# One attention prologue, reordered: a second key stack made by a selector product, queries earlier, the second block's keys later

## The chip, the core and the metric

The program runs on one core of a Trainium2 chip. The metric is the device time of one execution in microseconds. Before the change three runs gave 613.34, 617.55 and 617.87 us, median 617.55 us. One more execution was profiled: it took 615.51 us, its span in the trace is 613.8 us.

The core has five engines with queues of their own: TensorE (PE; its weight loads are PEld), VectorE (DVE), ScalarE (ACT), GpSimd (POOL) and SyncE (SP), which here does nothing but issue DMAs. They meet only through semaphores.

## The reference

The input is 2048 tokens of 128 features. Two layers each add an attention-like branch and an FFN-like branch to the layer norm of the input. The change lies at the start of layer 0, in the branch with 16 query heads, 4 key/value heads and a head width of 8:

```
xn = layernorm(x)                      # (x - mean) / sqrt(var + eps)
h  = rmsnorm(xn) * ln1
q, k, v = h @ Wqkv + bqkv              # 16, 4 and 4 heads of 8
q, k = rmsnorm(rope(q)) * qn, rmsnorm(rope(k)) * kn
out  = softmax(causal(q k' / sqrt(8))) v   # all 2048 tokens
...                                    # gate, output product, mixture of 8 experts
```

The chunk-summary branch of layer 0 reads the same xn. Everything behind (experts, the state-space layer, the last FFN) is not touched.

## The kernel before, in words

**Blocks.** The 2048 tokens are 16 tiles of 128, and 4 blocks of 4 tiles. SP loads x block by block (line 676); the third block's load is issued behind eight smaller ones.

**Prologue on DVE.** For each block: `statistics` (lines 1745, 1748: four BatchNorm statistics, four aggregations), then ACT takes the root of the variance (line 896), DVE inverts it (1754), and `normed` computes the four tiles `xn = (x - mean) * rstd` with one tensor_scalar each (1756). Two small products (1758, 1759) lead to a second root on ACT (898) for the RMS scale. PE transposes the four tiles (1214), ACT copies the result to `xnT` (902), and PE multiplies it with the weights (1220) once DVE has scaled these by ln1 (1787). `bound_of_scores` (1767 to 1775) computes a few constants from the norm weights. `block_taken` (1794) reads the products out of PSUM, one tile per instruction. `rotated`, `keys_split` and `split` apply the rotary tables and the norms and write each number as a high and a low part. All this stands in one written order on DVE.

**Stacks.** A score product has 32 rows of contraction (8 numbers, split in four), and four of them run side by side in the array. So the queries of a group (4 heads that share one key head) and four copies of its keys lie stacked on 128 partitions, in `qst` and `kst`. The queries come stacked out of a transpose (1252). The keys come as four groups on 32 partitions each (`keysT`, transposed at 1245, copied by ACT at 923), and must be repeated four times. For group 0 of block 0 a product with a 32 by 128 selector does that (1309), and ACT copies its result (925). For all other groups and blocks SP does it by DMA, four DMAs per group (`spread_keys`, 714): 12 for block 0, 16 for each later block. `keysT` is one buffer: the next block's keys may be copied there once the last block's DMAs have landed.

**Steps.** The attention is a list of 136 steps `k`: (group, query block, key tiles). Query block 0 is steps 0 to 9: group 0 has steps 0 and 1, group 1 steps 2 to 4, group 2 steps 5 and 6, group 3 steps 7 to 9. Block 1 begins at step 10, and from step 14 on it uses its own keys. Each step is two score pieces on PE (1335), two exponentials on ACT of 1024 columns each (965), a causal mask on POOL where the tiles are diagonal (843; all of steps 0 to 9), and the value product on PE two steps later (1354). The score pieces go around three pairs of PSUM banks. The value products of two groups accumulate in bank 6; before the next pair may start there (step 5's product, issued in step 7), DVE must have copied the bank out (2070).

**Side tasks.** Beside the steps, PE works through one list of other products that share bank 7, at most one at a time, each at a step given by the `ASKED` table: the query stacks of the next groups (QUERIES), the transpose of the next block's keys (KEYS), the transposed sums (ATT, 1437), the projections of blocks 2 and 3 (QKV). PE starts one only when the one before has been read out of the bank, nearly always by DVE (2187 for QUERIES, 2182 for KEYS, 2210 and 2215 for ATT). DVE has a list of events sorted by a step number: reading the side tasks, and the block's own norm and rotation work (squares 2086, sums 1807, roots 1892 to 1897, rotation 1815 to 1818, `keys_split` 1826 to 1834, `split` 1840 to 1842, the chunk means 1880 and 1882). Both lists are fixed when the program is written: an engine that reaches an entry early waits.

In the kernel before, the side tasks of the first steps are QUERIES of group 1 at step 0, of group 2 at step 2, of group 3 at step 4, KEYS of block 1 at step 5, ATT at step 7, QUERIES of block 1, group 0 at step 8. Step 2 waits until the 12 DMAs have landed.

## Time and profile before

| | |
|---|---|
| runs | 613.34, 617.55, 617.87 us |
| profiled execution | 615.51 us, span 613.8 us |
| PE busy | 560.9 us (91%) |
| ACT busy | 460.6 us (75%) |
| DVE busy | 399.9 us (65%) |
| POOL busy | 123.0 us (20%) |
| mean granted TensorE clock | 0.986 |

How to read it: the shares are means over the whole program. The change touches roughly the first 55 us of it; what it is worth is decided by who waits for whom there, and by whether the stages behind simply begin earlier.

### The profile page before, as it was taken

Reading aid. Unit: us, or ns where it says so; the run is one execution under the profiler, and the core shown is the slowest. Engines: PE = TensorE matmul, PEld = TensorE weight load, DVE = VectorE, ACT = ScalarE, POOL = GpSimd, SP = SyncE. Lnnn points to the kernel's source line nnn. Section 1 sums busy time; section 2 is a strip of 40 time slices with the busy share of each in tenths; the row PEclk is TensorE's granted clock in tenths of the full one; section 3 lists DMA queues with packets and bytes.
Section 4 is the critical chain, followed back from the end, with each engine's and each line's share of the span. In section 5 each row is a group of like instructions: output and inputs, shape, how many; then the busy total and the mean of one; then the engine's idle time right before and its main releaser. Section 6 shows DMA issues by size and latency. Waiting matters only on the chain.

```text
span 613.8 us, 11144 instructions
## 1 busy us (share of the span) xinstructions
PE 560.9 (91%) x3912; PEld 330.6 (54%) x3917; DVE 399.9 (65%) x1060; ACT 460.6 (75%) x642; POOL 123.0 (20%) x160
## 2 busy tenths in 40 slices
PE   4578989999999999999997899799689999999998
PEld 3233335344344333433334568467468887887887
DVE  7986765737445242576534855789689788788673
ACT  2368988898989999998794456559777687686673
POOL 2044221011101012010630545303011001010010
PEclk9879999999999999999899899999999999999999
DMA  7112002013422220040135331300000000000000
GB/s 230 27 43 70 2 1 70 1 32 95 172 92 105 104 88 18 2 139 1 45 100 161 114 88 40 94 1 2 0 1 1 2 18 1 2 18 1 1 18 18
DMA packets 31174, 30.98 MB, mean 50 GB/s; under 512 B 6912, under 2 KB 21024, under 8 KB 31120
## 3 DMA queue, kind: packets, MB, share of 16 engines
q1 hardware_dynamic: 29872, 27.71, 14.4%
q0 software_dynamic: 1248, 2.57, 1.2%
q8 instruction: 32, 0.52, 0.4%
q14 instruction: 22, 0.18, 0.1%
HBM read 13.44 MB, written 12.89 MB: 43 GB/s over the span
## 4 chain that ended last, share of the span: by engine, by line
PE 68%; DVE 19%; issue 5%; ACT 4%; DMA 2%; SPq 1%; POOL 1%; DVEq 0%; ACTq 0%; POOLq 0%
PE ps L1354 18%; PE ps L1335 8%; PE ps L92 5%; PE ps L94 5%; PE ps L93 5%; PE ps L1654 2%; PE ps L1418 2%; PE ps L1431 2%; PE ps L1252 1%; PE ps L1529 1%; PE ps L1692 1%; PE ps L1695 1%; PE ps L1423 1%; SPq L714 1%; ACT r L965 1%
## 5 line engine op out<-in xcount | busy, mean ns | idle before, releaser
L965 ACT ACTIVATE r<-ps 128x1024 f32<-128x1024 f32 x272 | 258.0, 1036 | 29.4 <-PE ps L1335 27.3
L1354 PE MATMUL ps<-r 128*32 128x512 f32 (+3 forms) x1280 | 146.5, 544 | 2.2 <-DVE r L2070 0.9
L843 POOL TENSOR_SCALAR_AFFINE_SELECT r<-r 128x512 f32<-128x512 f32 (+1 forms) x80 | 47.3, 593 | 219.2 <-ACT r L965 218.9
L1335 PE MATMUL ps<-r2r 32*128 32x512 f32 (+3 forms) x640 | 78.1, 451 | 6.2 <-DMA r2r<-r2r 4.3
L1335 PEld LDWEIGHTS ps<-r2r 32*128 32x128 f32 x640 | 34.4, 184 | 47.7 <-ACT r L965 18.8
L886 POOL TENSOR_TENSOR r<-r 128x512 f32<-128x512 f32 x16 | 22.1, 1382 | 151.5 <-ACT r L1163 130.5
L1354 PEld LDWEIGHTS ps<-r 128*32 128x32 f32 x1280 | 27.8, 108 | 42.3 <-issue 29.8
L94 PE MATMUL ps<-r2r 128*128 128x512 f32 (+1 forms) x104 | 39.0, 375 | 0.0
L93 PE MATMUL ps<-r2r 128*128 128x512 f32 (+1 forms) x88 | 32.8, 372 | 0.0
L861 POOL DMA_INDIRECT rows_by_token<-r x23 | 26.3, 1145 | 18.9 <-ACT r L1018 10.3
L92 PE MATMUL ps<-r1r 128*128 128x512 f32 x64 | 26.3, 411 | 1.7 <-DVE r2r L2482 1.5
L821 POOL DMA_INDIRECT rows_by_expert<-r x16 | 15.7, 984 | 58.0 <-DVE r L1994 54.1
L94 PE MATMUL ps<-r1r,r2r 128*128 128x512 f32 x64 | 25.2, 394 | 0.0
L93 PE MATMUL ps<-r2r,r1r 128*128 128x512 f32 x64 | 25.2, 394 | 0.0
L1141 ACT ACTIVATE r1r<-r 128x512 fp32r<-128x512 f32 x16 | 10.1, 629 | 19.7 <-DVE r L2430 19.5
L1148 ACT ACTIVATE r<-ps,row 128x512 f32<-128x512 f32 x16 | 11.0, 687 | 16.6 <-PE ps L94 16.1
L92 PE MATMUL ps<-r2r 128*128 128x512 f32 (+1 forms) x56 | 20.9, 373 | 1.6 <-DVE r2r L2387 1.1
L94 PEld LDWEIGHTS ps<-r2r 128*128 128x128 f32 x104 | 19.6, 188 | 3.8
L1232 PE MATMUL ps<-consts 128*128 128x512 bf16 x69 | 18.0, 400 | 3.3 <-DMA r<-rows_by_token 1.4
L2495 DVE TENSOR_SCALAR r<-ps,r 128x128 f32<-128x128 f32 x64 | 17.9, 343 | 3.9 <-PE ps L1674 3.9
L2187 DVE CAST r2r<-ps 128x512 fp32r<-128x512 f32 x15 | 10.4, 691 | 14.7 <-PE ps L1252 14.5
L2013 DVE SCALAR_TENSOR_TENSOR r<-r,ps 128x256 f32<-128x256 f32 x23 | 9.7, 420 | 15.2 <-ACT r L943 15.0
(403 smaller groups left out, 1190.2 us busy)
## 6 DMA issues: line engine op xcount, KB each, us to landing
rows_by_expert<-r SPq DMA_DIRECT2D x34, 258.0 KB, 2.5
r2r<-r2r SPq DMA_DIRECT2D x60, 64.0 KB, 2.0
r<-in_f_W SPq DMA_DIRECT2D x1, 2048.0 KB, 9.3
r<-rows_by_expert SPq DMA_DIRECT2D x23, 64.5 KB, 1.8
res<-in_x SPq DMA_DIRECT2D x4, 256.0 KB, 4.5
r<-in_g_h1T SPq DMA_DIRECT2D x1, 1024.0 KB, 5.6
r<-in_g_h2T SPq DMA_DIRECT2D x1, 1024.0 KB, 7.8
r<-rows_by_token SPq DMA_DIRECT2D x4, 256.0 KB, 3.8
```

The costliest lines, as they stand in the source:

```text
L92: pe.matmul(dst, wh, xh, start=start, stop=False)
L93: pe.matmul(dst, wh, xl, start=False, stop=False)
L94: return pe.matmul(dst, wl, xh, start=False, stop=stop)
L821: pool.indirect_dma_start(hbuf, bass.IndirectOffsetOnAxis(ap=slot_u[:, i:i + 1], axis=0), h2_rows[i], None).then_inc(s_scat, 16)
L843: pool.affine_select(blk, blk, pattern, ALU.is_ge, nothing, base=0, channel_multiplier=-1).then_inc(s_msk, 1)
L861: pool.indirect_dma_start(tbuf, bass.IndirectOffsetOnAxis(ap=token_u[:, t:t + 1], axis=0), ysb[:, t, :], None).then_inc(s_ysc, 16)
L886: pool.tensor_tensor(mm[:, b], ed[:, b], along(gm[:, b, :], NH), ALU.mult).then_inc(s_cm, 1)
L965: act.activation(probs[:, n % PBUFS, :, :], ps[:, b:b + 2, :], ACT.Exp).then_inc(s_exp, 1)
L1232: pe.matmul(ps[:, bank, :], busy_w, busy_x, start=True, stop=True)
L1335: m = pe.matmul(ps[:, 2 * (n % SBUFS) + h, at:at + TB - query], kst[32 * j:32 * j + 32, group, P * kt:P * kt + P], qst[32 * j:32 * j + 32, ...
L1354: m = pe.matmul(ps[32 * j:32 * j + 32, 6, query:TB], vp[:, kt, group, :], probs[:, (2 * v + j // 2) % PBUFS, j % 2, at:at + TB - query], s ...
L2495: dve.tensor_scalar(ed[:, b, h, :], ps[:, 1, P * h:P * h + P], cums_f[:, NH * i + h:NH * i + h + 1], 0.0, ALU.subtract, ALU.min).then_inc( ...
```

## The change

- **Normalisation moves from DVE to ACT.** DVE computes `negmean = -mean * rstd` for the four tiles of a block with one small instruction; ACT computes `xn = Identity(rstd * x + negmean)` tile by tile, four activations with a scale and a bias column each.
- **The weights are scaled by ln1 on ACT**, behind the roots of block 1.
- **`bound_of_scores` is cut into three pieces** at three places of DVE's order.
- **Second key stack.** The selector is built for 64 rows, and a second selector product makes the stack of group 1 in bank 5; ACT copies it. The DMAs of block 0 are 8 instead of 12, and the wait for them moves from step 2 to step 5. On PE the first key stack now comes ahead of the first query stack.
- **Order in the tail of the prologue.** DVE reads two tiles of block 1, copies the first query stack, then reads the other two.
- **Side tasks.** QUERIES of groups 1, 2, 3 at steps 0, 1, 3 (were 0, 2, 4); KEYS of block 1 at step 8 (was 5, now behind ATT); QUERIES of block 1, group 0 at step 9 (was 8); DVE's `split` of block 1 at 8.2 (was 6.4), which puts the first chunk means (8.1) ahead of it. From step 10 on both lists are as before.
- **Filler products** (`kept_busy`) ahead of step 0: one instead of five.

```diff
-        key_rows = lambda b: 16 * (NQ - REP) + 16 * NQ * b
+        key_rows = lambda b: 16 * (NQ - 2 * REP) + 16 * NQ * b
...
-            + [(at, 1, "KEYS", b, None, 0) for b, at in ((1, 5), (2, 25.5), (3, 48))]
-            + [(2 * g - 2, 1, "QUERIES", (0, g), None, 0) for g in range(1, NKV)]
+            + [(at, 1, "KEYS", b, None, 0) for b, at in ((1, 8), (2, 25.5), (3, 48))]
+            + [(at, 1, "QUERIES", (0, g), None, 0) for g, at in ((1, 0), (2, 1), (3, 3))]
...
-               ((1, (8, 12, 16, 19)), ...
+               ((1, (9, 12, 16, 19)), ...
...
-            spread_keys(0, range(1, NKV))
+            spread_keys(0, range(2, NKV))
...
-            at = slice(0, 32)
-            step.alone(pool.tensor_copy(selk[at].rearrange("p (j y) -> p j y", j=REP), along(ident[at, at], REP)))
+            for at in (slice(0, 32), slice(32, 64)):
+                step.mark(pool.tensor_copy(selk[at].rearrange("p (j y) -> p j y", j=REP), along(ident[at, at], REP)))
+            step.settle()
...  ACT, block_roots(b)
+                act.wait_ge(s_nm, b + 1)
+                for i in range(TPB * b, TPB * b + TPB):
+                    act.activation(xn[:, i, :], res[:, i, :], ACT.Identity, bias=negmean[:, i:i + 1],
+                                   scale=rstd[:, i:i + 1]).then_inc(s_xn, 1)
...  ACT, behind block_roots(1)
+            act.wait_ge(s_wqkv, 16 * 5)
+            act.activation(wqkv, wqkv, ACT.Copy, scale=ln1).then_inc(s_wsc, 1)
...  ACT, behind the copy of the first key stack
+            act.wait_ge(s_skt, 2)
+            act.activation(kst[:, 1, 0:TB], ps[:, 5, :], ACT.Copy).then_inc(s_skc, 1)
...  PE
-            pe.wait_ge(s_xnTc, 1)
-            pe.wait_ge(s_split, 1)
-            queries_transposed(0, 0).then_inc(s_sqt, 1)
-            kept_busy(5, 2)
+            def keys_stacked(bank, g):
+                return pe.matmul(ps[:, bank, :], selk[32 * g:32 * g + 32, :], keysT[32 * g:32 * g + 32, :],
+                                 start=True, stop=True)
             pe.wait_ge(s_kc, 1)
             pe.wait_ge(s_sel, 1)
             pe.wait_ge(s_xnTc, 2)
-            pe.matmul(ps[:, 1, :], selk[0:32, :], keysT[0:32, :], start=True, stop=True).then_inc(s_skt, 1)
+            keys_stacked(1, 0).then_inc(s_skt, 1)
+            pe.wait_ge(s_split, 1)
+            queries_transposed(0, 0).then_inc(s_sqt, 1)
+            keys_stacked(5, 1).then_inc(s_skt, 1)
...  PE, k == 0
-                        kept_busy(5, 3)
+                        pe.wait_ge(s_xnTc, 3)
+                        kept_busy(2, 1)
...  PE, k == 1
+                        pe.wait_ge(s_skc, 2)
-                    elif k == of_round(1, 0)[0]:
+                    elif k == of_round(2, 0)[0]:
                         pe.wait_ge(s_krep, key_rows(0))
...  DVE, normed(b)
-                for i in range(TPB * b, TPB * b + TPB):
-                    dve.tensor_scalar(xn[:, i, :], res[:, i, :], mv[:, i, 0:1], rstd[:, i:i + 1],
-                                      ALU.subtract, ALU.mult).then_inc(s_xn, 1)
+                dve.scalar_tensor_tensor(negmean[:, at], mv[:, at, 0], -1.0, rstd[:, at], ALU.mult, ALU.mult
+                                         ).then_inc(s_nm, 1)
...  DVE
-            dve.wait_ge(s_wqkv, 16 * 5)
-            dve.tensor_scalar(wqkv, wqkv, ln1, None, ALU.mult).then_inc(s_wsc, 1)
             statistics(2)
             scales(0)
+            bound_of_scores(0)
             normed(2)
-            bound_of_scores()
...
             statistics(3)
+            bound_of_scores(1)
             normed(3)
             rotated(0, 1)
+            bound_of_scores(2)
...
-            block_taken(1)
+            block_taken(1, range(0, 2))
             dve.wait_ge(s_sqt, 1)
             dve.tensor_copy(qst[:, 0, 0:TB], ps[:, 0, :]).then_inc(s_sqc, 1)
+            block_taken(1, range(2, 4))
...
-            split_at.update({1: 6.4, 2: 24.6})
+            split_at.update({1: 8.2, 2: 24.6})
```

## Rows read from the trace of the kernel before

**Rows 1.** The page, chain of work that ended last, share of the span by engine.

```profile
PE 68%; DVE 19%; issue 5%; ACT 4%; DMA 2%; SPq 1%; POOL 1%; DVEq 0%; ACTq 0%; POOLq 0%
```

**Rows 2.** Timeline of ACT: start us, us, engine, line, operation, tiles, count, idle before.

```profile
31.23 3.77 ACT L965 ACTIVATE r<-ps 128x1024 f32<-128x1024 f32 x4 [0.64 <-PE ps L1335]
37.94 1.94 ACT L965 ACTIVATE r<-ps 128x1024 f32<-128x1024 f32 x2 [2.94 <-PE ps L1335]
...
54.92 22.79 ACT L965 ACTIVATE r<-ps 128x1024 f32<-128x1024 f32 x24 [0.15 <-PE ps L1335]
```

**Rows 3.** Third load of x: timeline of SP, then the DMA view (KB, us to landing).

```profile
4.78 0.99 SPq L676 DMA_DIRECT2D res<-in_x  x2
...
res<-in_x SPq DMA_DIRECT2D x1, 256.0 KB, 5.3
```

**Rows 4.** Timeline of the prologue, all engines.

```profile
10.31 0.87 DVE L1745 BATCH_NORM_STATS2 stats<-res 128x6 f32<-128x128 f32 x4
...
11.04 2.90 PE L1220 MATMUL ps<-r,xnT 128*128 128x192 f32 x8 [0.60 <-ACT xnT L902]
...
14.62 1.39 DVE L1794 SCALAR_TENSOR_TENSOR r<-ps,small,row 128x192 f32<-128x192 f32 x4
...
20.65 1.12 DVE L1756 TENSOR_SCALAR xn<-res,small 128x128 f32<-128x128 f32 x4
...
21.68 0.15 DVE L1758 TENSOR_TENSOR small<-small 128x4 f32<-128x4 f32 x1
```

**Rows 5.** ACT groups by form: count, busy us, mean ns, idle before us.

```profile
L1073 ACT ACTIVATE r<-r,row 128x512 f32<-128x512 f32 x5 | 3.9, 802 | 0.0
...
L955 ACT ACTIVATE r<-ps 128x128 f32<-128x128 f32 x5 | 1.4, 275 | 2.6 <-PE ps L1295 2.6
```

**Rows 6.** Timeline of the hand-over from prologue to steps.

```profile
27.85 0.42 DVE L1842 CAST r1r<-r1r 128x512 fp32r<-128x512 f32 x1
28.07 7.60 SPq L714 DMA_DIRECT2D r2r<-r2r  x12
...
31.13 0.66 PE L1252 MATMUL ps<-consts,r1r 128*128 128x128 f32 x4
...
31.89 0.69 DVE L2187 CAST r2r<-ps 128x512 fp32r<-128x512 f32 x1 [0.98 <-PE ps L1252]
```

**Rows 7.** Timeline of DVE in the first steps.

```profile
40.92 0.69 DVE L2187 CAST r2r<-ps 128x512 fp32r<-128x512 f32 x1 [1.17 <-PE ps L1252]
...
47.04 0.69 DVE L2187 CAST r2r<-ps 128x512 fp32r<-128x512 f32 x1
...
49.96 0.69 DVE L2070 COPY r<-ps 128x512 f32<-128x512 f32 x1 [0.79 <-PE ps L1354]
...
53.20 0.49 DVE L2215 TENSOR_TENSOR r<-ps,r 128x128 f32<-128x128 f32 x2
```

**Rows 8.** Timeline of PE and of SP: second spread, steps 10 and 14.

```profile
49.26 10.71 SPq L714 DMA_DIRECT2D r2r<-r2r  x16
...
50.70 1.06 PE L1354 MATMUL ps<-r 128*32 128x512 f32 x8 [0.21 <-DVE r L2070]
...
55.82 0.68 PE L1335 MATMUL ps<-r2r 32*128 32x512 f32 x4
...
63.83 0.51 PE L1335 MATMUL ps<-r2r 32*128 32x512 f32 x4
```

**Rows 9.** Windows: stretch, us, PE, PEld, DVE, ACT, POOL busy, PEclk, DMA.

```profile
34.50:35.00 0.50, 0.00 (x0) 0.00 (x0) 0.47 (x2) 0.50 (x1) 0.30 (x1) 0.68 0.39 98
...
41.00:41.50 0.50, 0.50 (x11) 0.28 (x12) 0.50 (x1) 0.00 (x0) 0.00 (x0) 0.50 0.00 0
```

**Rows 10.** Timeline of PE after the DMA wait.

```profile
37.10 0.80 PE L1335 MATMUL ps<-r2r 32*128 32x512 f32 x4 [4.29 <-DMA r2r<-r2r]
37.83 1.93 PE L1354 MATMUL ps<-r 128*32 128x512 f32 x8
```

**Rows 11.** Timeline of DVE: one operation of `keys_split`, block 0 and block 1.

```profile
25.63 0.29 DVE L1830 TENSOR_TENSOR r<-r,row 128x128 f32<-128x128 f32 x1
...
44.28 0.61 DVE L1830 TENSOR_TENSOR r<-r,row 128x128 f32<-128x128 f32 x1
```

More of the change, by code:

```diff
@@ L306, in build @@
         roots = small[:, 32:64].rearrange("p (q a i) -> p q a i", q=NB, a=2)
+        negmean = small[:, 112:128]
         inverse = small[:, 64:96].rearrange("p (q a i) -> p q a i", q=NB, a=2)
@@ L533, in build @@
             [(at + 2 * n, 2, "QKV", (b, n), None, 0) for b, at in ((2, 10), (3, 14)) for n in range(2)]
-            + [(at, 1, "KEYS", b, None, 0) for b, at in ((1, 5), (2, 25.5), (3, 48))]
-            + [(2 * g - 2, 1, "QUERIES", (0, g), None, 0) for g in range(1, NKV)]
+            + [(at, 1, "KEYS", b, None, 0) for b, at in ((1, 8), (2, 25.5), (3, 48))]
+            + [(at, 1, "QUERIES", (0, g), None, 0) for g, at in ((1, 0), (2, 1), (3, 3))]
             + [(at, 1 if b < 2 else 2, "QUERIES", (b, g), ("KEYS", b), 1) for b, steps in
-               ((1, (8, 12, 16, 19)), (2, (25.6, 33, 45, 52)), (3, (65, 74, 89, 102))) for g, at in enumerate(steps)]
+               ((1, (9, 12, 16, 19)), (2, (25.6, 33, 45, 52)), (3, (65, 74, 89, 102))) for g, at in enumerate(steps)]
             + [(27, 4, "KV", 0, ("KEYS", 2), 0), (26, 4, "GMAT", 0, ("KV", 0), 2), (31, 4, "G0", 0, ("KV", 0), 2),
@@ L1764, in scales, with bound_of_scores @@
                 step.alone(dve.reciprocal(hs[:, at], sd2[:, at]))
-            def bound_of_scores():
-                step.alone(dve.tensor_tensor(kw, qn_bc, kn_bc, ALU.mult))
-                step.mark(dve.tensor_scalar(kw, kw, QD ** -0.5, None, ALU.mult))
-                step.mark(dve.tensor_reduce(mx2[:, 0:1], qn_bc, X_AXIS, ALU.max, apply_absolute_value=True))
-                step.mark(dve.tensor_reduce(mx2[:, 1:2], kn_bc, X_AXIS, ALU.max, apply_absolute_value=True))
-                step.settle()
-                step.alone(dve.tensor_tensor(shift, mx2[:, 0:1], mx2[:, 1:2], ALU.mult))
-                step.alone(dve.tensor_scalar(shift, shift, -(QD ** 0.5), None, ALU.mult))
-                step.mark(dve.memset(qhl_f[:, :, :, 1, 1, 0], 1.0))
-                step.mark(dve.tensor_copy(khl[:, :, :, 1, 1, 0], shift.unsqueeze(2).broadcast_to([P, TPB, NKV])))
+            def bound_of_scores(piece):
+                if piece == 0:
+                    dve.wait_ge(s_wqkv, 16 * 5)
+                    step.mark(dve.tensor_tensor(kw, qn_bc, kn_bc, ALU.mult))
+                    step.mark(dve.tensor_reduce(mx2[:, 0:1], qn_bc, X_AXIS, ALU.max, apply_absolute_value=True))
+                    step.mark(dve.tensor_reduce(mx2[:, 1:2], kn_bc, X_AXIS, ALU.max, apply_absolute_value=True))
+                elif piece == 1:
+                    step.mark(dve.tensor_scalar(kw, kw, QD ** -0.5, None, ALU.mult))
+                    step.mark(dve.tensor_tensor(shift, mx2[:, 0:1], mx2[:, 1:2], ALU.mult))
+                else:
+                    step.mark(dve.memset(qhl_f[:, :, :, 1, 1, 0], 1.0))
+                    step.alone(dve.tensor_scalar(shift, shift, -(QD ** 0.5), None, ALU.mult))
+                    step.mark(dve.tensor_copy(khl[:, :, :, 1, 1, 0], shift.unsqueeze(2).broadcast_to([P, TPB, NKV])))
                 step.settle()
@@ L1844, in split, with block_taken @@
                 dve.sem_inc(s_split, 1)
-            def block_taken(b):
-                for i in range(TPB):
+            def block_taken(b, tiles=range(TPB)):
+                for i in tiles:
                     dve.wait_ge(s_qkvp, TPB * b + i - i % 2 + 2)
```

1 line of the change is left out of this document (added).

## The prediction

> **What bounds the kernel now.** I read the chain of waits first: PE holds 68% of it and DVE 19% [rows 1]. Followed through the first 60 us the chain is almost all DVE up to the first key transpose, then the key DMAs, then PE and DVE in turn; so I read the timelines of these 60 us engine by engine. ACT tells where the attention loses time. The first exponential starts at 31.23, number 18 at 54.92. From there 24 of them take 22.79 us, 0.95 each; 18 of them would take 17.1 us, but 23.7 passed, so ACT waited 6.6 us. The largest wait is 2.94 us, for step 2 [rows 2]. PE names its cause: 4.29 us idle until the key DMAs landed [rows 10]. The 12 DMAs are issued 0.633 us apart from 28.07 [rows 6]; the last starts at 35.04 and PE goes on at 37.10, so a DMA lands 2.06 us after its issue.
>
> The rest of the 6.6 us is DVE's. Between its copy of the second query stack (ends 32.58) [rows 6] and that of the fourth (ends 47.73) it waited 1.17 us in all [rows 7]: 15.15 - 1.17 = 13.98 us of work. I take this number as the core of the forecast.
>
> **The change, part by part.**
>
> *Normalisation to ACT, blocks 0 and 1.* DVE loses four instructions (1.12 us) per block and gains one of the kind that takes 0.15 [rows 4]. But the third block of x lands at 4.78 + 5.3 = 10.1, and DVE began its statistics at 10.31 [rows 3, 4]: at most 0.2 us can come out of the two blocks. ACT's price shows nowhere at this size. Below it is a plain 128-column activation, 0.275, above it one of 512 columns with scale and bias, 0.802 [rows 5]. It is nearer to the first; I take 0.38 a tile, 1.5 us a block. The Trainium skill (ScalarE: Activation LUTs, What ACT_TABLE_LOAD costs) gives 186 ns + 0.833 N, 93 ns more for each pointer operand, 93 ns of overlap: by that an estimate of 0.39 a tile and 1.54 us a block; the 512-column row fits it (0.80), and the sum would not move. ACT then ends block 1 at about 10.0, its second root at 10.2, the scaled weights at 10.5 and the copy of block 0's features at 11.1. So PE starts the projection at about 11.15 instead of 11.04 and ends it 2.90 us later, at 14.05 [rows 4].
>
> *Reading the projection.* DVE came to it at 14.62 and took 1.39 us, to 16.01 [rows 4]. It will now be there before PE: the last pair of tiles is read after 14.05, done at 14.85. Gain 1.15 us.
>
> *From there to `split`.* Block 3's normalisation: 1.12 out, 0.15 in, less what overlapped, 0.8 out. The pieces of `bound_of_scores`: the first lies ahead of a wait for ACT, the second inside one, the third costs about 0.45. So `split` of block 0, which ended at 28.27 [rows 6], ends 1.15 + 0.8 - 0.45 = 1.5 us earlier, at 26.77. From both sides: 0.7 if ACT takes 0.45 a tile and holds the projection back, 2.5 if PE has block 0 ready sooner.
>
> *Hand-over.* Two tiles of block 1 are read ahead of the query stack and two behind it. The key stack of group 1 costs PE 0.5 us and ACT 0.6 us, both inside DVE's 1.4 us of reads and copy. Counting from 26.77: scale and two tiles 0.95, query copy 0.7, two tiles 0.7, transpose 0.7 with its hop, copy of the second query stack 0.75: it ends at 30.6, against 32.58. The gain is now 2.0 us. Step 0's exponential starts near 29.0 instead of 31.23.
>
> *The DMA wait.* Eight DMAs from 26.5: the last lands at 26.5 + 7 x 0.633 + 2.06 = 33.0. Step 5 comes at 29.0 + 10 x 0.95 = 38.5 at the earliest. This wait, 4.29 us of PE, goes to nothing, and the half clock behind it with it. If the DMAs were not covered, the price would be the same 4.29 us at step 5.
>
> **What is late next** is DVE. With the wait gone ACT could run the exponentials back to back from 29.0; number 16 (step 8) would be due at 44.2. DVE has the same 13.98 us of work as before: the second, third and fourth query stacks, the norm work of block 1, its values. Moving QUERIES and KEYS changes its order, not its amount. And it is slowed: operations of `keys_split` took 0.29 in block 0 and 0.61 in block 1, where POOL masks at the same time [rows 11]. Before, POOL had nothing to mask during the 4.29 us; now it masks through all of it, some three masks more, for which I add 0.5 us (nothing, if they fall between; 2 us if each small operation meets one). By the Trainium skill (SBUF — State Buffer, Who interferes with whom) an exclusive lock makes a DVE instruction with two SBUF inputs wait for a GpSimd instruction that reads SBUF; that rule speaks against the change and would put it nearer to the 2 us. So DVE has finished block 1's values at 30.6 + 14.0 + 0.5 = 45.1 and copied bank 6 at 45.85, instead of 50.65 [rows 7]. That is a gain of 4.8 us there, but the value product of step 5 (in step 7) now waits for this copy some 3 us instead of 0.21 [rows 8].
>
> *KEYS behind ATT.* Now the ping-pong, PE and DVE in turn, each with 0.05 for the hop. Value product 1.06 [rows 8], transpose of ATT 0.66 [rows 6], to 47.65; meanwhile DVE reads ATT, 0.95 (two products, 0.49 [rows 7], and two reciprocals), while PE does step 8's scores and a value product, to 49.1; KEYS transpose to 49.75; copy to 50.5. SP starts the second spread at 50.55, **1.3 us later than before** (49.26) [rows 8]. Its 16 DMAs: before, 10.71 us of issue and 2.06 from the last, so landed at about 61.35; now at 62.65. Step 14 needs them, and began at 63.83 [rows 8]: it had 2.4 us to spare. Now it can begin at 62.7. Gain 1.1 us.
>
> *`split` behind the chunk means.* 50.5 + 0.65 + 1.7, transpose and copy 1.4: block 1's first queries at 54.35, step 10 at 54.4 instead of 55.82 [rows 8]. Gain 1.4 us; four steps of 2.0 us later that asks for step 14 at 62.4, so the DMAs end last, narrowly.
>
> From step 14 on both lists are the same and everything waits for something else in the list; nothing there waits for a time. The 1.1 us go through to the end. **Sum: 615.51 - 1.1 = 614.4 us** for an execution like the profiled one. The three runs have their median 2.04 us above it; the four executions together have the mean 616.1, less 1.1 is **615.0 us**, which I predict.
>
> **The rivals.**
>
> *The clock falls in the new wait (slower).* The granted clock fell to 0.50 (1.2 GHz) at about 34.7, 1.9 us into PE's wait for the DMAs, and stayed there until 41.5, 4.4 us after PE had gone on [rows 9, 10]; the value product took 1.93 instead of 1.06 [rows 8, 10]. The new wait of some 3 us in step 7 is of that kind. It decides if the granted clock stands at 0.50 when bank 6 has been copied. Then, from 45.9: value product 1.93, ATT 1.12, scores 0.8, value product 1.6, KEYS 0.7, copy 0.7, to 52.7, which is 2.2 us later: step 14 begins at 64.95, **1.1 us later than before: 616.6 us**. For it: the length of the wait. Against it: PE is busy up to it, while before it stood nearly idle in the first steps. Chance 0.27.
>
> *DVE is not the bound (faster).* If the norm work of block 1 shrinks without the stalls around it, or PE's pauses in fact cost the time, KEYS comes in step 8 as ACT paces it: transposed at 46.2, copied at 46.9, landed at 59.0, step 14 at 59.05. Gain 4.8 us, **610.7 us**. Against it: the 13.98 us hold no wait. Chance 0.13.
>
> *The prologue does not get shorter.* ACT becomes what DVE was: 1.5 us a block plus roots and the hop, with the features and the weights queued behind. Then the 2.0 us of the hand-over are lost, all of the rest stands, and 1.1 turns to -0.9: **616.4 us**. Chance 0.1.
>
> **How the numbers follow.** The forecast has 0.5, the rivals 0.27, 0.13 and 0.1. All four lie within 0.8% of each other, less than the 613.34 to 617.87 of the runs. The low end of the range is the fast rival, 610.7. The high end is the slow one, 616.6, plus the 1.8 us by which the highest run stands above the mean: 618.4. A measurement of this kernel tells about 1% (6.2 us) from no change. Faster by that needs the fast rival and more, or runs that fall well: 0.07. Slower by that needs the slow rival with a spread that lands after step 14 by more than another 4 us: 0.04. Within 1%: 0.89.
>
> **What would show it.** Right: no wait of PE for key DMAs at step 2 or 5; first exponential near 29.0; exponentials back to back to about number 14; then PE waiting 2 to 4 us for the copy of bank 6, second spread starting at or after 49.3, step 14 at 62 to 63.5. Slow rival: clock 0.50 after 45. Fast rival: second spread before 48. Wrong altogether would be a first exponential later than 31.2, or a gain at step 14 that the end of the span does not show.

## The result and the profile after

The changed kernel took 619.36 us (median of 11 runs, 618.46 to 620.52), the kernel before, on the same chip, 614.32 us (11 runs). The ratio is **1.0064, 95% interval 1.0045 to 1.0084: slower by 0.6%**. The forecast was 615.0 and the range ended at 618.4, so the time lies outside it. The profiled execution took 619.21 us with a span of 617.1, 3.3 us more than the 613.8 of before. Its chain of waits, by engine, answers to [rows 1]:

```profile
PE 67%; DVE 20%; issue 5%; ACT 5%; DMA 1%; POOL 1%; DVEq 0%; ACTq 0%; POOLq 0%
```

The shares hardly move: the difference arises in the first 67 us. The prologue did what was forecast. These are rows from the timelines of several engines (start us, us, engine, line); they answer to [rows 3, 4, 6]:

```profile
5.89 1.65 ACT L902 ACTIVATE xn<-res,small 128x128 f32<-128x128 f32 x4 [0.44 <-DVE small L1771]
...
26.06 0.42 DVE L1858 CAST r1r<-r1r 128x512 fp32r<-128x512 f32 x1
...
26.76 34.99 SPq L716 DMA_DIRECT2D r2r<-r2r  x24
...
30.06 0.69 DVE L2206 CAST r2r<-ps 128x512 fp32r<-128x512 f32 x1 [0.52 <-PE ps L1263]
...
44.97 0.69 DVE L2089 COPY r<-ps 128x512 f32<-128x512 f32 x1
```

`split` ends at 26.48 (forecast 26.77, before 28.27), the second query stack is copied at 30.75 (30.6; 32.58), bank 6 at 45.66 (45.85; 50.65). ACT's timeline answers to [rows 2]:

```profile
29.19 12.94 ACT L976 ACTIVATE r<-ps 128x1024 f32<-128x1024 f32 x14 [0.27 <-PE ps L1351]
44.35 1.94 ACT L976 ACTIVATE r<-ps 128x1024 f32<-128x1024 f32 x2 [2.22 <-PE ps L1351]
49.39 3.96 ACT L976 ACTIVATE r<-ps 128x1024 f32<-128x1024 f32 x4 [3.10 <-PE ps L1351]
57.19 1.94 ACT L976 ACTIVATE r<-ps 128x1024 f32<-128x1024 f32 x2 [3.84 <-PE ps L1351]
60.73 1.94 ACT L976 ACTIVATE r<-ps 128x1024 f32<-128x1024 f32 x2 [1.59 <-PE ps L1351]
```

Fourteen exponentials run back to back from 29.19, as forecast, and the wait of 2.94 us for step 2 is gone. Then come four waits, 10.8 us together; before, there were three up to step 10 (2.94, 1.70 and 1.73 us), 6.4 together. PE's timeline says what each is (it answers to [rows 8, 10]):

```profile
43.52 0.80 PE L1351 MATMUL ps<-r2r 32*128 32x512 f32 x4 [2.58 <-DVE r2r L2206]
...
45.72 1.94 PE L1370 MATMUL ps<-r 128*32 128x512 f32 x8 [1.40 <-DVE r L2089]
47.59 1.12 PE L1453 MATMUL ps<-consts,r 128*128 128x128 f32 x4
...
54.95 0.63 PE L1263 MATMUL ps<-consts,r1r 128*128 128x128 f32 x4 [2.56 <-DVEq L1860]
56.36 0.80 PE L1351 MATMUL ps<-r2r 32*128 32x512 f32 x4 [0.78 <-DVE r2r L2206]
57.09 1.94 PE L1370 MATMUL ps<-r 128*32 128x384 f32 x16
...
59.89 0.80 PE L1351 MATMUL ps<-r2r 32*128 32x512 f32 x4
60.62 1.93 PE L1370 MATMUL ps<-r 128*32 128x256 f32 x16
...
63.14 0.50 PE L1351 MATMUL ps<-r2r 32*128 32x512 f32 x4
...
67.05 0.51 PE L1351 MATMUL ps<-r2r 32*128 32x512 f32 x4
```

In step 7 PE waits 2.58 us for DVE's copy of the fourth query stack and 1.40 more for bank 6: the forecast's "some 3 us". In step 9 it waits 2.56 us for `split` of block 1, then 0.78 for the copy of that stack; this second place the prediction did not have. DVE was idle shortly before it came to that `split`:

```profile
48.74 0.37 DVE L2229 RECIPROCAL r<-ps 128x16 f32<-128x16 f32 x2 [3.07 <-PE ps L1453]
```

It stood 3.07 us until PE had transposed ATT, and 1.35 more until PE had transposed KEYS, with the 2.2 us of `split` behind both in its order. The rotation that `split` reads had ended at 42.74.

Behind each of PE's two places of waiting the value product takes 1.94 instead of 1.06 or 1.07. Step 10 begins at 56.36 and step 14 at 67.05 (before 55.82 and 63.83). The windows (stretch, us, busy time of PE, PEld, DVE, ACT, POOL, granted clock, DMA share, GB/s) answer to [rows 9]:

```profile
42.00:43.00 1.00, 0.00 (x0) 0.00 (x0) 0.96 (x2) 0.13 (x1) 0.86 (x2) 0.65 0.03 8
43.00:49.00 6.00, 4.08 (x20) 1.58 (x24) 2.57 (x10) 1.94 (x2) 1.05 (x3) 0.50 0.00 0
49.00:50.00 1.00, 1.00 (x20) 0.47 (x20) 0.60 (x3) 0.61 (x1) 0.00 (x0) 0.93 0.00 0
55.00:56.00 1.00, 0.57 (x4) 0.33 (x4) 0.39 (x1) 0.00 (x0) 0.69 (x3) 0.98 0.35 88
56.00:57.00 1.00, 0.64 (x4) 0.29 (x4) 1.00 (x3) 0.00 (x0) 0.00 (x0) 0.50 0.50 125
57.00:62.00 5.00, 5.00 (x42) 1.98 (x38) 0.49 (x1) 3.21 (x4) 0.00 (x0) 0.50 0.42 104
62.00:63.00 1.00, 1.00 (x10) 0.43 (x2) 0.38 (x1) 0.66 (x1) 0.00 (x0) 0.61 0.30 76
```

The granted clock falls twice in these 67 us, and PE has work for nearly all of the second stretch at 1.2 GHz. From step 10 to step 14 PE needs 10.69 us; before it needed 63.83 - 55.82 = 8.01. Step 14 is 3.2 us late, and the span is 3.3 us longer: what is lost at step 14 arrives at the end, as the prediction's last step had it for a gain. The ratio is 3.9 us, with 2.8 to 5.2 as its interval, and holds the 3.2.

### The profile page after: what moved, and what is told of

It is laid out like the page before. It is cut to its first block, busy times and chain, and to the rows that moved or that the text cites. A ratio compares the mean times of both kernels' runs of the same rounds, so it can differ in the third digit from the quotient of the medians.

```text
span 617.1 us, 11140 instructions
## 1 busy us (share of the span) xinstructions
PE 566.2 (92%) x3909; PEld 331.6 (54%) x3914; DVE 397.0 (64%) x1047; ACT 467.7 (76%) x660; POOL 124.8 (20%) x161
## 4 chain that ended last, share of the span: by engine, by line
PE 67%; DVE 20%; issue 5%; ACT 5%; DMA 1%; POOL 1%; DVEq 0%; ACTq 0%; POOLq 0%
PE ps L1370 17%; PE ps L1351 8%; PE ps L92 5%; PE ps L94 5%; PE ps L93 5%; PE ps L1670 2%; PE ps L1434 2%; PE ps L1447 2%; PE ps L1263 1%; PE ps L1545 1%; PE ps L1708 1%; PE ps L1711 1%; PE ps L1231 1%; PE ps L1439 1%; ACT r L976 1%
## 5 line engine op out<-in xcount | busy, mean ns | idle before, releaser
L1370 PE MATMUL ps<-r 128*32 128x512 f32 (+3 forms) x1280 | 148.3, 551 | 3.3 <-DVE r L2089 2.1
L1351 PE MATMUL ps<-r2r 32*128 32x512 f32 (+3 forms) x640 | 79.5, 454 | 5.7 <-DVE r2r L2206 4.1
L824 POOL DMA_INDIRECT rows_by_expert<-r x16 | 17.8, 1111 | 58.0 <-DVE r L2013 54.1
L864 POOL DMA_INDIRECT rows_by_token<-r x23 | 24.5, 1063 | 18.7 <-ACT r L1029 10.1
L2179 DVE TENSOR_TENSOR r<-ps,r 128x512 f32<-128x512 f32 (+1 forms) x11 | 7.1, 643 | 19.2 <-PE ps L1434 19.2
## 6 DMA issues: line engine op xcount, KB each, us to landing
r<-rows_by_expert SPq DMA_DIRECT2D x23, 64.5 KB, 1.8
```

The costliest lines, as they stand in the source:

```text
L864: pool.indirect_dma_start(tbuf, bass.IndirectOffsetOnAxis(ap=token_u[:, t:t + 1], axis=0), ysb[:, t, :], None).then_inc(s_ysc, 16)
L1351: m = pe.matmul(ps[:, 2 * (n % SBUFS) + h, at:at + TB - query], kst[32 * j:32 * j + 32, group, P * kt:P * kt + P], qst[32 * j:32 * j + 32, ...
L1370: m = pe.matmul(ps[32 * j:32 * j + 32, 6, query:TB], vp[:, kt, group, :], probs[:, (2 * v + j // 2) % PBUFS, j % 2, at:at + TB - query], s ...
```

## The experiments

A mark that all kernels share makes them comparable: the start of step 14. In fifteen of eighteen profiles a transpose of ATT near 152 us follows it by 88.55 to 88.60 us, so nothing between depends on the change (the three exceptions are told at the end). The stretch from step 14 to the end of the span varies more, from 548.6 to 550.1 us in nine profiles without added work, and is 554 to 559 us on two slower chips. The times of whole executions are compared as ratios to the kernel before, run in turn with it on the same chip.

| kernel | step 10 | step 14 | ratio, 95% interval |
|---|---|---|---|
| before | 55.82 | 63.83 | 1 |
| the change | 56.36 | 67.05 | 1.0064, 1.0045 to 1.0084 |
| the change, again | 57.11 | 66.45 | 1.0058, 1.0038 to 1.0078 |
| steps' part alone | 57.78 | 68.42 | 1.0074, 1.0046 to 1.0101 |
| change, both waits filled | 54.30 | 62.12 | 0.9967, 0.9941 to 0.9993 |
| the same, again | 54.24 | 62.06 | 0.9968, 0.9951 to 0.9986 |
| filled in step 7 only | 54.15 | 63.46 | 1.0014, 0.9992 to 1.0036 |
| filled in step 9 only | 57.28 | 65.11 | 1.0007, 0.9990 to 1.0024 |
| DVE's order changed | 55.22 | 65.25 | 0.9999, 0.9979 to 1.0019 |
| the same, filled | 55.66 | 63.48 | 1.0007, 0.9991 to 1.0023 |
| prologue's part alone | 53.80 | 61.80 | 0.9971, 0.9939 to 1.0003 |
| the same, DMA wait filled | 53.33 | 61.33 | 0.9971, 0.9949 to 0.9994 |
| change, old side tasks | 53.24 | 61.24 | 0.9983, 0.9959 to 1.0006 |
| the same, KEYS wait filled | 53.71 | 61.71 | 0.9931, 0.9912 to 0.9950 |
| the same kernel, again | 55.29 | 63.29 | 0.9969, 0.9956 to 0.9983 |
| old side tasks, both filled | 52.96 | 60.96 | 0.9956, 0.9939 to 0.9974 |

"Filled" means filler products (`kept_busy`) where PE would wait: they keep it at work on a bank whose content nobody needs at that time, and compute nothing of the result.

### What the two falls cost

**The change with both waits filled.** The edit, in the steps' loop, ahead of the value product that starts bank 6 again, and ahead of the first query stack of block 1:

```diff
+                    if k in (7, 10):
+                        pe.wait_ge(s_exp, 2 * k - SBUFS + 1)
+                        kept_busy(2 * (2 * k % SBUFS), 10 if k == 7 else 3)
...
+                        if n == 1:
+                            kept_busy(SHARED, 5)
...
+                        if which == (1, 0):
+                            kept_busy(SHARED, 10)
```

> The changed kernel with filler products in PE's four new waits (10 in a score bank ahead of step 7's query stack, 5 in the shared bank ahead of the copy of bank 6, 10 ahead of the split of step 9, 3 ahead of step 10); nothing else changed. Theory 1, the clock: the changed kernel loses because PE's granted clock falls to 0.50 twice, at 42.3 and at 56.1. Then both falls go, step 7's value product takes 1.06 instead of 1.94, ATT 0.66 instead of 1.12, steps 10 and 11 take 2.0 us each instead of 3.5 and 3.3; step 14 moves from 67.05 to about 62.8, the span from 617.1 to about 613, a ratio to before of 0.997 to 1.0. Rival, DVE alone: PE waits for DVE whatever its clock, the falls are only a sign of it. Then step 14 stays beyond 65.5 and the span above 615.5.

Measured: 619.67 us, ratio 0.9967 (0.9941 to 0.9993). PE's timeline of the filled kernel, and its windows:

```profile
40.63 2.11 PE L1243 MATMUL ps<-consts 128*128 128x512 bf16 x9 [0.16 <-issue]
43.05 0.50 PE L1354 MATMUL ps<-r2r 32*128 32x512 f32 x4 [0.32 <-DVE r2r L2213]
43.49 1.25 PE L1243 MATMUL ps<-consts 128*128 128x512 bf16 x5
45.26 1.06 PE L1375 MATMUL ps<-r 128*32 128x512 f32 x8 [0.52 <-DVE r L2096]
...
52.86 0.66 PE L1263 MATMUL ps<-consts,r1r 128*128 128x128 f32 x4 [0.20 <-DVEq L1867]
...
54.30 0.51 PE L1354 MATMUL ps<-r2r 32*128 32x512 f32 x4
54.74 1.07 PE L1375 MATMUL ps<-r 128*32 128x384 f32 x16
...
62.12 0.50 PE L1354 MATMUL ps<-r2r 32*128 32x512 f32 x4
```

```profile
43.00:49.00 6.00, 5.42 (x53) 2.44 (x56) 2.72 (x13) 3.56 (x4) 1.34 (x3) 1.00 0.01 3
56.00:62.00 6.00, 6.00 (x52) 2.23 (x51) 1.34 (x3) 5.95 (x7) 0.00 (x0) 1.00 0.36 90
```

The granted clock is 1.00 in both stretches, the value products take 1.06 and 1.07 again, steps 10 to 14 need 7.82 us. Nothing was removed: DVE's waits are still PE's waits, only PE spends them at work. Step 14 comes 4.9 us earlier than in the change, as theory 1 had it (62.8 or so), and not beyond 65.5. The falls behind the waits, not the waits, are the loss.

**The same again, on another chip**, beside the version with the lowest times below. (The edit is the one above.)

> The changed kernel with fillers in both of its waits, a second time and on the same chip as the kernel beside it. Theory: as its first run, step 10 at 54.3, step 14 at 62.1, ratio 0.9972 (1.7 us over 616). Rival (its first ratio was the chip's scatter): ratio 1.000 or above at the same step times.

Measured: 614.00 us, ratio 0.9968 (0.9951 to 0.9986), step 14 at 62.06: the first ratio again.

**Each wait filled alone**, and **the change once more**, all on one chip. The first keeps of the edit above what bears on step 7 (`k == 7` and `n == 1`), the second what bears on step 9 (`k == 10` and `which == (1, 0)`), the third has no edit.

> The changed kernel with the filler products of step 7 alone (10 and 5). Theory 1 (each fall has its own price): the first fall goes, 1.6 us of it; the waits behind step 9 (3.3 us) stand and the clock falls there, which costs about 2.9 us over steps 10 to 12: step 14 at 65 to 65.7, ratio 1.002 to 1.004. Rival (only the first fall counts, it brings the second): step 14 below 63.5, ratio below 0.999, like e1_fill.

> The changed kernel with the filler products behind step 9 alone (10 and 3). Theory 1: the first fall stays with its 1.6 us, the second goes with its 2.9: step 14 at 63.7 to 64.5, ratio 0.999 to 1.002. Rival (only the first fall counts): step 14 beyond 65.5, ratio as the change, 1.006.

> The changed kernel, nothing else, on the chip of the next three, so that they can be set against it. Theory 1: again two falls of the clock behind the prologue, in or behind step 7 and behind step 9, step 14 at 66.5 to 67.5, ratio 1.004 to 1.009. Rival (where the falls come is chance, and the loss with them): step 14 below 65.5 in this execution.

Measured: 616.01 us (1.0014), 615.82 us (1.0007) and 619.04 us (1.0058). The timelines of PE, step 7 filled first, then step 9 filled:

```profile
45.05 1.06 PE L1375 MATMUL ps<-r 128*32 128x512 f32 x8 [0.52 <-DVE r L2094]
...
52.74 0.63 PE L1263 MATMUL ps<-consts,r1r 128*128 128x128 f32 x4 [2.56 <-DVEq L1865]
54.15 0.80 PE L1354 MATMUL ps<-r2r 32*128 32x512 f32 x4 [0.78 <-DVE r2r L2211]
```

```profile
45.55 1.94 PE L1373 MATMUL ps<-r 128*32 128x512 f32 x8 [1.70 <-DVE r L2094]
...
55.84 0.66 PE L1263 MATMUL ps<-consts,r1r 128*128 128x128 f32 x4 [0.20 <-DVEq L1865]
...
57.28 0.51 PE L1354 MATMUL ps<-r2r 32*128 32x512 f32 x4
```

With the first fall left in (second fence) step 10 comes at 57.28 instead of 54.30: 3.0 us, and steps 10 to 14 take 7.83. With the second fall left in (first fence) step 10 is on time, 54.15, and steps 10 to 14 take 9.31: 1.5 us more. In the change itself this stretch took 10.69, in its second profile 9.34. So **the first fall costs about 3 us and the second 1.5 to 2.9**, and each alone is what separates a small gain from no change. The intervals of the two half-filled kernels include 1; that of the filled one does not. I had expected 1.6 us for the first fall and 2.9 for the second, so step 14 at 65 or later with step 7 filled and at 64.5 at the latest with step 9 filled; 63.46 and 65.11 came, the dearer fall being the first.

### Could DVE's order do it without fillers?

The fourth query stack is copied before bank 6, and the rotation of block 1 stands ahead of both. This kernel asks DVE for both copies first:

```diff
-            + [(at, 1, "QUERIES", (0, g), None, 0) for g, at in ((1, 0), (2, 1), (3, 3))]
+            + [(at, 1, "QUERIES", (0, g), None, 0) for g, at in ((1, 0), (2, 1), (3, 2))]
...
-            rotated_at[1] = [1.5, 2.8]
+            rotated_at[1] = [1.5, 6.1]
...
-            keys_split_at = {1: (2.9, 3.0), ...
+            keys_split_at = {1: (7.1, 7.2), ...
```

(the last values of block 1 go from 3.6 to 9.2 and the first chunk means from 8.1 to 9.1).

> The changed kernel with another order of the same DVE work, no filler: the fourth query stack is asked for at step 2 instead of 3; DVE copies it and bank 6 ahead of the second half of the rotation (6.1), keys_split (7.1, 7.2) and the values (9.2) of block 1; the first chunk means come behind the queries of block 1 (9.1). Theory 1 (PE's waits for DVE in step 7 are what brings the first fall of the clock): the waits of step 7 go, KEYS of block 1 is copied at 47.5 to 48.5 instead of 51.67, step 14 at 60.5 to 62, ratio to before 0.995. Rival (the total of DVE's work decides, the order does not): the wait only moves to KEYS and the split, as long in all, the clock falls there, step 14 beyond 64, ratio 1.0 or more.

Measured: 622.39 us, ratio 0.9999 (0.9979 to 1.0019). PE's timeline:

```profile
49.55 0.69 PE L1256 MATMUL ps<-consts,r2r 128*128 128x128 f32 x4 [2.71 <-DVEq L1852]
53.35 1.09 PE L1263 MATMUL ps<-consts,r1r 128*128 128x128 f32 x4 [0.51 <-DVEq L1860]
55.22 0.80 PE L1351 MATMUL ps<-r2r 32*128 32x512 f32 x4 [0.78 <-DVE r2r L2206]
```

The wait in step 7 has gone and stands again, 2.71 us long, in front of the KEYS transpose (its `keys_split` is what now comes late); the clock fell behind it and the queries of block 1 took 1.09 instead of 0.66. My theory for this run, that this order ends the falls, fell; its rival, that a wait of DVE's size only moves, was right. **With the fillers added** at these places:

> The order of e3_order and the filler products of e1_fill together. Theory 1: no fall of the clock between step 0 and step 14, and the keys of block 1 leave 3 us earlier than in the changed kernel: step 14 at 60.5 to 61, ratio 0.994 to 0.996, the fastest so far. Rival (the fillers delay PE more than they save, now that the waits are short): slower than e3_order by 0.5 us or more.

Measured: 622.55 us, ratio 1.0007 (0.9991 to 1.0023), step 14 at 63.48, granted clock 1.00 throughout, and a wait of 2.41 us for KEYS still there, this time with no fall behind it. Both expectations missed: step 14 was to come at 60.5 to 61, and the rival wanted it slower than without fillers. The second spread starts at 51.55, 1.8 us later than in the filled change, but step 14 does not wait for it: step 10 is already 1.4 us late (55.66 against 54.30), and from there to step 14 it is 7.82 us in both. Some 0.6 us of the 1.4 come from the fillers themselves: `split` had ended at 53.64, and they kept PE from the queries until 54.28. So this says only that late keys with these fillers bring nothing. An order that puts `split` of block 1 alone ahead of ATT and KEYS, where DVE was idle, was not run.

### Which part of the change gains, which loses

**The prologue's part alone**: normalisation and weights on ACT and `bound_of_scores` in pieces, but one key stack, 12 DMAs and the old side tasks. **The steps' part alone**: the rest, without these.

```diff
+                    act.activation(xn[:, i, :], res[:, i, :], ACT.Identity, bias=negmean[:, i:i + 1],
+                                   scale=rstd[:, i:i + 1]).then_inc(s_xn, 1)
...
+            bound_of_scores(0)
...
```

> The kernel before with the prologue part alone: normalisation and weight scaling on ACT, the constants in three pieces; key stacks, DMAs and side tasks as before. Theory 1 (the prologue part is a gain and the rest loses it): keys_split ends 1.3 us earlier, the 12 DMAs land at about 35.8 instead of 37.06, and 1.3 us come through to the end: span 612.5, ratio 0.998. Rival (the prologue part loses or does nothing): span 613.8 or more.

> The kernel before with all of the change but the prologue part: second selector product, 8 DMAs, new side tasks, new order in PE's hand-over. Theory 1: the waits of PE at steps 7 and 9 and both falls of the clock stay, and the 1.3 us of the prologue are missing: span 618 to 619, ratio 1.008. Rival (the falls of the clock depend on where the steps fall in time, and a shift of 1.3 us may save one): span 615 to 616.

Measured: 619.11 us, ratio 0.9971 (0.9939 to 1.0003), and 626.52 us, ratio 1.0074 (1.0046 to 1.0101). The prologue's part keeps the DMA wait whole (PE idle for 4.29 us, until 35.09), with the clock at 0.51 from 34 to 41, and still has step 14 at 61.80, 2.0 us ahead of the kernel before: the forecast's 2.0 us of the hand-over, all of them. The steps' part has no wait for DMAs, and step 14 at 68.42; besides the two falls its profile has one more from 30 to 37 us, which the changed kernel's does not have. So the part that removes the large wait is the one that loses.

**The prologue's part with its DMA wait filled:**

```diff
+                        pe.wait_ge(s_exp, 2 * k - SBUFS + 1)
+                        kept_busy(2 * (2 * k % SBUFS), 14)
                         pe.wait_ge(s_krep, key_rows(0))
```

> The kernel before with the prologue part of the change (as e5_prologue_only) and 14 filler products in PE's wait for the 12 key DMAs at step 2. Theory 1: the clock does not fall there, the half-speed value products and transposes behind the wait (1.94 and 1.12) go, DVE gets its third query stack 1.2 us sooner and no longer waits for it; step 14 at 60.5 to 61, ratio 0.994 to 0.996, the fastest. Rival (DVE's own work sets the pace there): step 14 at 61.5 to 61.8 as in e5_prologue_only, ratio 0.997.

Measured: 613.88 us, ratio 0.9971 (0.9949 to 0.9994).

```profile
31.31 3.20 PE L1240 MATMUL ps<-consts 128*128 128x512 bf16 x14 [0.42 <-ACT r L973]
36.12 0.51 PE L1345 MATMUL ps<-r2r 32*128 32x512 f32 x4 [1.61 <-DMA r2r<-r2r]
...
45.28 0.66 PE L1253 MATMUL ps<-consts,r2r 128*128 128x128 f32 x4 [2.01 <-DVE r2r L2199]
```

The clock stayed at 1.00 from 26 to 62, and the gain at step 14 is 0.5 us (61.80 to 61.33), nothing in the ratio: my theory (60.5 to 61, 0.994 to 0.996) fell, its rival held. The DMAs landed 1.0 us later in this execution (PE goes on at 36.12, not 35.09), so it may hide a little, but not much: in the unfilled kernel DVE waited only 1.17 us for PE behind the fall, here 0.43, and no more than that 1.17 could be won. PE in turn waits 2.01 us for DVE later, instead of 1.07. The fall cost little here because DVE, not PE, was next on the path.

**The change with the old side tasks** (QUERIES at 0, 2, 4; KEYS at 5; block 1 at 8; `split` at 6.4):

```diff
-            + [(at, 1, "KEYS", b, None, 0) for b, at in ((1, 8), (2, 25.5), (3, 48))]
+            + [(at, 1, "KEYS", b, None, 0) for b, at in ((1, 5), (2, 25.5), (3, 48))]
...
-            split_at.update({1: 8.2, 2: 24.6})
+            split_at.update({1: 6.4, 2: 24.6})
```

> The changed kernel with the side tasks where they were before (QUERIES at 0, 2, 4, KEYS of block 1 at 5, QUERIES of block 1 at 8, split at 6.4). Theory 1 (any long wait for DVE drops the clock): DVE's work is the same, so the fourth query stack is copied at about 45.3 instead of 47.7 of before, but PE stands for 4 us or more in step 5 and the clock falls there once; step 14 at 61.5 to 63.5, span 611.5 to 613.5, better than the changed kernel by 4 us or more, since the keys of block 1 leave early and only one fall is left. Rival (the order of the tasks hardly matters): span within 1 us of 617.1.

Measured: 621.03 us, ratio 0.9983 (0.9959 to 1.0006), step 14 at 61.24 against 67.05. The reordering of the side tasks, not the second stack, carries the loss. Which of the four moves in it does, is open: they were only taken back together. I had expected one fall; there were two, near 31 to 38 us, with no wait of PE of 0.75 us or more ahead of it, and near 45 to 49. The fillers in its KEYS wait (2.55 us), in two runs of one kernel:

```diff
+                        kept_busy(4, 2)
...
+                        if what == "KEYS" and which == 1:
+                            pe.wait_ge(s_exp, 2 * (k + 1) - SBUFS + 1)
+                            kept_busy(2 * (2 * (k + 1) % SBUFS), 12)
```

> The kernel of e2_old_tasks (changed kernel, side tasks as before) with two filler products in step 1 and twelve in the wait of step 5. In e2_old_tasks the clock was low over most of steps 2 to 4 and again around steps 5 to 7, step 14 stood at 61.24. Theory 1 (clock): both go, and step 14 moves to about 60, ratio 0.995 to 0.997 against 0.998. Rival (here DVE alone sets the pace, PE's clock costs nothing): step 14 within 0.3 us of 61.24.

> The kernel of e7_old_tasks_fill once more. If its 0.9931 was real: 0.992 to 0.9945 again, and something behind step 14 is faster too. If it was scatter: 0.9955 to 0.998, as its step 14 says.

Measured: ratio 0.9931 (0.9912 to 0.9950) in 6 runs, then 0.9969 (0.9956 to 0.9983) in 12. The profile speaks for the second: 12 fillers ran at half clock (a fall had come from the wait for the stack before, 2.68 us) and held the KEYS transpose up. I take 0.9969; the first interval was too narrow for what it measured.

**Both waits of that table filled.** The first try:

```diff
-                        if what == "KEYS" and which == 1:
+                        if which == 1 or which == (0, 3):
...
-                            kept_busy(2 * (2 * (k + 1) % SBUFS), 12)
+                            kept_busy(2 * (2 * (k + 1) % SBUFS), 12 if which == 1 else 10)
```

> The kernel of e7_old_tasks_fill with ten more filler products in step 4, where PE waits for the copy of the third query stack. Theory 1 (the clock): it no longer falls between steps 0 and 14, the twelve fillers of step 5 end before DVE is ready, the KEYS transpose comes at 44.5 instead of 45.73, step 14 at 60.3 to 60.8, ratio 0.993 to 0.996 and the fastest of all. Rival (DVE sets the pace): step 14 at 61.2 or later, no better than e12_prologue_fill.

Measured: 633.35 us, ratio 1.0288 (1.0270 to 1.0306). The groups by line show why, this kernel first, then the next one:

```profile
L1243 PE MATMUL ps<-consts 128*128 128x512 bf16 x185 | 45.6, 391 | 4.8 <-DMA r<-rows_by_token 1.6 <-ACT r L976 1.0 <-DMA rows_by_token<-r 1.0
```

```profile
L1243 PE MATMUL ps<-consts 128*128 128x512 bf16 x94 | 24.5, 405 | 2.9 <-DMA r<-rows_by_token 1.6 <-DMA rows_by_token<-r 1.0 <-ACT r L1029 0.4
```

My condition held for every side task with the number 1, so some 91 fillers stood in places without a wait: 21.1 us of PE more; one and the same ATT transpose comes at 344.88 here and at 324.40 in the next kernel, 20.5 us later. It was an error of mine, but it gives a number: fillers where PE is the bound cost nearly their full time. The second try names the two tasks:

```diff
+                        if (what, which) in (("KEYS", 1), ("QUERIES", (0, 3))):
```

> The old side-task table with the new prologue, and fillers in two places alone: 12 ahead of the second KEYS transpose and 10 ahead of the transpose of the fourth query stack. (In the kernel before this one the same condition also put 12 fillers ahead of eight later side tasks; 107 fillers more at 0.38 us are 41 us of PE work, of which about 18 showed.) Theory (the clock is what turned the change's gain to a loss; with no fall, DVE's list alone sets the time): no fall behind the prologue, value product behind the fourth query stack 1.07 instead of 1.94, step 10 near 51.9, step 14 near 59.8, second spread near 45.3. Against before, whose step 14 began at 63.83, that is 4.0 us, ratio 0.9935. Rival (DVE and DMAs behind step 14 take the gain back, as the spread of the runs could hide so far): ratio 0.9965 or above, with step 14 still at 59.8.

Measured: 613.46 us, ratio **0.9956 (0.9939 to 0.9974)**.

```profile
37.09 2.33 PE L1243 MATMUL ps<-consts 128*128 128x512 bf16 x10
39.84 0.66 PE L1263 MATMUL ps<-consts,r1r 128*128 128x128 f32 x4 [0.42 <-DVE r2r L2210]
...
41.87 2.76 PE L1243 MATMUL ps<-consts 128*128 128x512 bf16 x12
44.92 0.66 PE L1256 MATMUL ps<-consts,r2r 128*128 128x128 f32 x4 [0.29 <-DVE r2r L2210]
...
47.84 1.07 PE L1371 MATMUL ps<-r 128*32 128x512 f32 x8 [0.21 <-DVE r L2093]
```

No fall behind the prologue; step 14 at 60.96, 2.9 us before the kernel before, and 2.7 us (0.44% of 616) in the ratio. The 4.0 us that I had expected did not come: step 10 began at 52.96, not near 51.9 (in the first try it stood at 53.38); and the 107 fillers of 41 us in that text should be about 91 of 21. That the gain passes through to the end holds. This version has the lowest time on its chip and the lowest ratio but for the 0.9931 above; the intervals of the filled change and of the filled prologue overlap with its own, so it is not shown to be the best of them. All three are faster than both kernels; the interval of the unfilled prologue version just includes 1.

### What DVE pays for POOL's masks

This kernel leaves out the causal masks of steps 0 to 9, so its result is another one; it ran once, and its time is not compared:

```diff
-                    pool.affine_select(blk, blk, pattern, ALU.is_ge, nothing, base=0, channel_multiplier=-1
-                                       ).then_inc(s_msk, 1)
+                    if k < of_round(0, 1)[0]:
+                        pool.sem_inc(s_msk, 1)
...
```

> The changed kernel without POOL's causal masks in steps 0 to 9 (20 of 80; POOL only counts up): this part of the computation is left out. It shows what DVE's work costs without POOL beside it. Theory 1 (the masks hold DVE's instructions with two inputs): from the copy of the second query stack to that of bank 6 DVE takes 13 us or less instead of 14.9, and the first wait of PE in step 7 shrinks by that. Rival (no contention): 14.9 us as before.

```profile
30.95 0.69 DVE L2209 CAST r2r<-ps 128x512 fp32r<-128x512 f32 x1 [0.98 <-PE ps L1266]
...
43.65 0.69 DVE L2092 COPY r<-ps 128x512 f32<-128x512 f32 x1
```

DVE needs 44.34 - 31.64 = 12.70 us from the copy of the second query stack to that of bank 6; in the change it needs 45.66 - 30.75 = 14.91. The masks cost it 2.2 us, with the same instructions. The stretched ones are mostly those with two inputs in SBUF: one rotation operation took 1.08 us with the masks and 0.76 without, the 640-column product 1.01 and 0.82, and with one input a tensor_scalar 0.41 and 0.20. The sum took 1.28 and 1.25, the copies out of PSUM 0.69 in both. Without the masks PE waited 0.80 us in step 7, and the clock did not fall there.

## Why the prediction was wrong, step by step

Two steps failed. "Value product 1.06", behind the new wait in step 7, took the clock to stay up; it fell, the product took 1.94, and the fall cost 3.0 us. And step 10 was reckoned without a wait of PE for `split`; PE stood 2.56 + 0.78 us, the clock fell again, and that cost 1.5 to 2.9 us more.

- **Normalisation to ACT, reading the projection, `split`, hand-over: right.** Four tiles took 1.65 us (I took 1.5; the estimate from the Trainium skill, ScalarE: Activation LUTs, What ACT_TABLE_LOAD costs, was 1.54, and the trace is near it), PE's projection of 2.90 us began at 10.93 (11.15), `split` ended at 26.48 (26.77), the second query stack was copied at 30.75 (30.6). Alone this part brings step 14 to 61.80, 2.0 us earlier.
- **The DMA wait: right.** It is gone at steps 2 and 5.
- **DVE is late next: right.** Bank 6 copied at 45.66 (45.85). The amount was 14.91 us to that copy's end (14.0 + 0.5 + 0.75 = 15.25). Of the masks I said 0.5 more than before. Up to the start of bank 6's copy DVE worked 14.22 us, 0.24 more than the 13.98 of before; the same work took 12.01 without masks. So the masks had cost some 2.0 us before already and cost 2.2 now. The prediction's rule from the Trainium skill (SBUF — State Buffer, Who interferes with whom) would have it nearer to 2 us more, which did not come; that most of the stretched operations have two inputs in SBUF agrees with it, and the runs do not show by which mechanism they were held up.
- **The new wait in step 7: right in its size, wrong in its owner and its consequence.** I had 3 us before the value product; 2.58 of it came a moment earlier, in front of step 7's scores, for the fourth query stack, and 1.40 behind. The step that failed is "Value product 1.06", with the 0.66 for the transpose of ATT behind it: the forecast (0.5) let PE stand about 3 us and go on at full speed. **The clock fell, which was the slow rival (0.27).** Its 2.2 us at KEYS came nearly true: KEYS was copied at 51.67, in the filled kernel at 49.68, 2.0 us earlier.
- **`split` behind the chunk means: a wait put at nothing, in forecast and rival.** I priced this move by its time alone: queries at 54.35, step 10 at 54.4. In the filled kernel it began at 54.30. But I never asked how long PE would stand: DVE has the KEYS copy (0.7), the chunk means (0.7) and `split` (2.2, where I had 1.7) to do, PE runs out of work in the middle of it and waits 2.56 us, then 0.78. That is a second wait of the first one's kind, and it meets the list where PE is the bound: steps 10 to 12 at half clock, 2.9 us. With it the rival fits: its step 10 comes at 54.4 + 2.2 = 56.6 (measured 56.36), and with the 10.69 us measured behind it step 14 at 67.3 (67.05). In time that is 615.51 + 3.5 = 619.0. That 619.36 lies so near is partly luck: 615.51 was one execution, and the kernel before had its median at 614.32 in the runs beside the change. The sums also stood on two bases: the forecast on the mean of 616.1, the rivals and the low end of the range on 615.51; on the mean the slow rival would be 617.2.
- **The second spread ends last: wrong, harmless.** In the filled kernel its 16 DMAs took 10.02 us of issue (10.71 before), from 49.76; in the changed kernel its issues end at 61.75 (51.75 + 10.00), and step 14 comes at 67.05.
- **From step 14 on nothing changes: right,** to 0.05 us at the mark near 152 us in fifteen profiles; to the end of the span, to 1.5 us.
- **The forecast's world exists.** With PE kept at work step 10 comes at 54.30 (54.4), step 14 at 62.12 (62.7), a gain of 1.7 us (1.1), in the ratio 0.9967 and 0.9968. The sum was good, two misses of its terms aside (0.24 for 0.5, and a second spread at 49.76 for 50.55); the choice of case was not, and the case chosen against had half of its price.
- **The chances.** Faster 0.07, same 0.89, slower 0.04 at 1%: it came within 1%. The range failed at the top, since the rival that set it had one fall.

## What to carry to other kernels

When a large wait of the matrix engine is taken away, write down where it will wait next and for how long, place by place, and price what follows each such wait at half clock: the price is large where the engine is the bound behind it (here 1.5 to 3 us a fall) and small where another engine is (0.5, at most 1.2 us, behind a wait of 4.29). Filler products in a wait that cannot be removed bring this back, as long as they end before the wait does; they held PE up by 0.6 us where they ended later, and cost nearly their full time where there was no wait (20.5 us for some 91). Look as well at what the other engine does just before: here DVE was idle for 3.07 us with the work that PE later waited for still ahead of it. And split a change in parts on the chip: here one part was worth 2 us, and the other took some 5.

## What the runs showed of the hardware

- Waits of nearly the same length ended differently. The clock fell in or behind waits of 4.29, 2.58 + 1.40 (1.70 in the second profile of the change), 2.55, 2.68 and 2.71 us, 1.29 + 2.02 (steps' part), 2.56 + 0.78, and 1.81 + 0.78 (without masks); it stood at 1.00 through single waits of 2.41, 2.01, 1.61 and 1.60 us. In four profiles (steps' part, old side tasks, DVE's order changed, without masks) it also stood near 0.50 for some microseconds between 29 and 38 us, with no wait of PE of 0.75 us or more in these steps; all four ran on the two slower chips, and the changed kernel itself had no such fall in either profile. Where it had fallen, PE first did work at half clock before it rose (value products of 1.94).
- The granted clock also falls in places that no kernel here changes, and not in each execution: near 105 us in two profiles (the change with old side tasks, and step 7 filled), which puts the transposes at 152 us 1.5 us further behind step 14 than in the other kernels; and between 295 and 365 us in all but one of them (step 7 filled). Falls like that near 105 us, 1.5 us each, are part of the spread of single executions. The third kernel in which step 14 does not tell the rest is the one with fillers everywhere.
- Two profiles of one kernel (old side tasks, KEYS wait filled) have step 14 at 61.71 and 63.29, the change has 67.05 and 66.45: what differs is when a fall begins and how long it lasts (in the first pair 0.73 in the window 40 to 42 us and 0.50 in the next, against 0.77 from 38 to 40 and 0.50 to 0.53 up to 46). A conclusion from one profile on less than 1.5 us needs the ratio beside it.
- Two of the chips were slower in all kernels alike (the kernel before 620.75 and 622.21 us against 614.32 to 616.22). It lies mostly behind step 14: 554 to 559 us from there to the end of the span, against 549 to 550.
